# Routing and dispatch of the first mixture moved into the first attention, with the squared query norms as one fp32 product

## What is computed

```python
# first attention: 16 heads of 128
q = rmsnorm((layernorm(x) @ Wq).reshape(B, Sq, 16, 128), gq)
k = rmsnorm((ctx @ Wk).reshape(B, 64, 16, 128), gk)
v = (ctx @ Wv).reshape(B, 64, 16, 128)
x = x + tanh(g_xattn[0]) * softmax(q @ k.T * scale) @ v @ Wo
# first mixture: 64 experts, 8 a token, at most 128 tokens an expert (CAP)
n = layernorm(x)
scores = sigmoid(n @ router.T)
sc = scores + e_bias                      # 8 groups of 8 experts
# keep the 4 groups whose two best sc have the largest sum,
# then the 8 best experts in them; weights: scores / their sum * 2.5
pos = how many earlier (token, choice) pairs chose this expert
buf[expert, pos] += n[token]              # only where pos < CAP
y = (silu(buf @ w_gate) * (buf @ w_up)) @ w_down
x = x + tanh(g_ffn[0]) * (sum of weight * y of each token's experts + shared_mlp(n))
```

## Time and profile before

| | us |
|---|---|
| median of 3 runs | 1334.66 (1333.32 to 1339.74) |
| the profiled execution | 1336.93 |
| its span | 1335.2 |
| busy PE, DVE, ACT, POOL | 1038.4 (78%), 697.9 (52%), 431.5 (32%), 278.2 (21%) |
| DMA packets, moved | 58967, 66.36 MB |

### The profile page before, as it was taken

The page is one execution under the profiler, slowest core; times in us unless marked ns, Lnnn a source line. Parts: engine busy times, 40 slices in busy tenths (PEclk is TensorE's granted clock), DMA queues, the critical chain, the costliest instruction groups (busy, mean ns, idle before and its releaser), DMA issues.

```text
span 1335.2 us, 16322 instructions
## 1 busy us (share of the span) xinstructions
PE 1038.4 (78%) x5301; PEld 855.8 (64%) x5301; DVE 697.9 (52%) x1659; ACT 431.5 (32%) x793; POOL 278.2 (21%) x223
## 2 busy tenths in 40 slices
PE   5989979989766400776667368887989999999997
PEld 3867858778545300665556226564657989898996
DVE  6277586675758897222223477575675324232221
ACT  4565465554623100111111032324252232322221
POOL 0414214133000001788787110010100000000000
PEclk8999999999887655888787566757666999899899
DMA  7004000000001040788786540000000000000001
GB/s 266 3 0 137 1 1 1 0 1 1 1 0 40 24 126 11 170 173 180 166 186 120 144 164 1 2 0 0 0 0 0 1 1 0 0 0 0 0 0 64
DMA packets 58967, 66.36 MB, mean 50 GB/s; under 512 B 5037, under 2 KB 55719, under 8 KB 58151
## 3 DMA queue, kind: packets, MB, share of 16 engines
q1 hardware_dynamic: 45268, 46.48, 11.1%
q0 software_dynamic: 12288, 18.88, 8.1%
q10 hardware_dynamic: 1363, 0.37, 0.1%
HBM read 48.13 MB, written 17.56 MB: 49 GB/s over the span
## 4 chain that ended last, share of the span: by engine, by line
PE 54%; DVE 14%; issue 12%; DMA 6%; ACT 6%; POOL 6%; ACTq 0%; DVEq 0%; POOLq 0%; SPq 0%
PE bank L1959 12%; PE bank L1978 7%; DMA acc<-y,dst_now 5%; PE bank L1619 4%; PE bank L1664 4%; PE bank L1887 3%; PE bank L1845 3%; PE bank L1649 3%; POOL acc L489 2%; PE bank L1970 2%; POOL xg L479 2%; PE bank L1904 2%; POOL q_lo L468 2%; DVE cand L901 1%; PE bank L1804 1%
## 5 line engine op out<-in xcount | busy, mean ns | idle before, releaser
L1959 PE MATMUL bank<-gu_hi,xnT_split 128*128 128x352 f32 x640 | 158.7, 328 | 0.0
L468 POOL TENSOR_TENSOR q_lo<-soft,q_hi 128x512 fp32r<-128x512 f32 x64 | 93.2, 1456 | 236.8 <-ACT soft L1313 236.7
L1959 PEld LDWEIGHTS bank<-gu_hi,xnT_split 128*128 128x128 f32 x640 | 112.6, 190 | 1.0 <-issue 0.7
L479 POOL DMA_INDIRECT xg<-table,src_now x64 | 63.9, 999 | 216.5 <-DVE src_now L927 197.4
L489 POOL DMA_INDIRECT acc<-y,dst_now x64 | 102.3, 1599 | 26.7 <-issue 20.3
L1959 PE MATMUL bank<-gu_lo,xnT_split 128*128 128x352 f32 x320 | 103.8, 324 | 0.0
L1183 DVE SCALAR_TENSOR_TENSOR soft<-sg,combine_w,bank 128x176 f32<-128x176 f32 x160 | 56.4, 395 | 87.4 <-PE bank L1959 81.3
L1978 PE MATMUL bank<-dn,attnT 128*128 128x256 f32 x448 | 101.2, 384 | 0.0
L1978 PEld LDWEIGHTS bank<-dn,attnT 128*128 128x128 f32 x448 | 85.6, 194 | 11.2
L707 DVE COPY qT<-bank 128x512 f32<-128x512 f32 x64 | 44.2, 691 | 87.7 <-PE bank L1664 86.6
L1517 ACT ACTIVATE sg<-bank 128x352 f32<-128x352 f32 x80 | 37.1, 464 | 152.0 <-PE bank L1959 151.9
(11 more groups left out here) (256 smaller groups left out, 2140.1 us busy)
## 6 DMA issues: line engine op xcount, KB each, us to landing
w_gu<-in_L_ffn_w_gu SPq DMA_DIRECT2D x32, 352.0 KB
w_dn<-in_L_ffn_w_down SPq DMA_DIRECT2D x32, 176.0 KB
acc<-zeros SPq DMA_DIRECT2D x2, 2176.0 KB, 11.4
acc_rows<-acc SPq DMA_DIRECT2D x8, 512.0 KB, 4.9
gu<-in_L_gu SPq DMA_DIRECT2D x1, 3520.0 KB, 13.7
table<-xw SPq DMA_DIRECT2D x4, 640.0 KB
wo<-in_L_xattn_Wo SPq DMA_DIRECT2D x2, 1024.0 KB, 16.2
wq<-in_L_xattn_Wq SPq DMA_DIRECT2D x1, 2048.0 KB, 18.5
```

The source lines that it names most:

```text
L468: pool.tensor_tensor(q2_lo[:, h % 3, :], q2[h % 2], q2_hi[:, h % 3, :], ALU.subtract).then_inc(q2_split, 1)
L479: pool.indirect_dma_start(xg[:, q, e, :], None, table, bass.IndirectOffsetOnAxis(ap=src_now[:, q, e:e + 1], axis=0)).then_inc(xg_loaded[q] ...
L1959: mm = pe.matmul(b[:, 0:2 * F1], v[:, c, j * P:(j + 1) * P], w[:, c, p, o, :], start=(n == 0), stop=(n == len(terms) - 1))
```

## The change

In the first attention:

- the squares are made once, in fp32, and the squared norm is one fp32 product a half (two of 256 columns a head). `band_r`, `q2_hi`, `q2_lo` and POOL's subtraction are gone;
- the keys are copied by ACT, which also squares them in PSUM with a running sum (16 squares of 128 columns), in place of DVE's copy, product and sum;
- the values of group i-1, and the transposes of the keys of group i, stand inside step i;
- the 16 tiles are routed in nine batches (tile 0; 1 and 2; ... ; 15), each with a layer norm (`ln_stats`, `ln_roots`, `ln_apply`), a choice (`choose1` to `choose3`) and a place (`place`). In step i a batch `early(i)` is normed and chosen, a batch `late(i)` is normed at the step's end, chosen in step i+1, and both are placed in step i+1. Five batches (4 to 8) are placed after the last step;
- a chosen row's slot is found by a product with a triangle of ones (`earlier`) and the counts so far (`taken`), so that the search by `largest` is gone. POOL then writes each row to its slot in `table` by indirect DMAs without accumulation: eight a tile, 128 in all (`send_rows`), with a number column that names the token;
- the sigmoid is made of an exponential on ACT and a reciprocal on DVE;
- the table has 8192 slots and is filled with blank rows first (10.5 MB by SP's queue in step 0, beside the zeroed accumulators);
- normed tokens also go to DRAM (`normed_T`) and return for the shared expert, which is computed after the last place.

In the expert stage SP loads the rows of a pair with one direct DMA in place of POOL's two gathers, weights come in longer pieces (2816 bytes and 2048 bytes a partition, by a new layout made on the host, in place of 704 and 1024), and the next loads of a slot wait for `y_ready` in place of `y_full`.

The diff, cut to its core:

```diff
-                    act.activation(q2_hi[:, h % 3, :], qT[:, h % 3, :], ACT.Square)
...
-                for half in range(2):
...
-                        for n, v in enumerate((q2_hi, q2_lo)):
-                            mm = pe.matmul(n_bank[0:H0, at], band_r[:, H0 - 1 - row:2 * H0 - 1 - row],
-                                           v[:, h % 3, at], start=(h == half == n == 0),
+                        mm = pe.matmul(n_bank[0:H0, at], band[:, H0 - 1 - row:2 * H0 - 1 - row], q2[h % 2][:, at],
+                                       start=(h == half == 0), stop=(h == H0 - 1 and half == 1))
...
+BATCHES = [[0]] + [[2 * n - 1, 2 * n] for n in range(1, NT // 2)] + [[NT - 1]]
+def early(i):
+    return 2 * (i - 1)
+def late(i):
+    return 2 * i - 1
...
+            ROUTE_LATE = {1: (place, -1), 3: (choose1, 0), 4: (choose2, 0), 5: (choose3, 0), 9: (place, 0)}
+            ROUTE_EARLY = {8: ln_stats, 9: ln_roots, 10: ln_apply, 13: choose1, 14: choose2, 15: choose3}
...
+                    if i and h == 0:
+                        key_norm(i)
...
+                        if h == 12:
+                            row_stats(i + 1)
+                        elif h == 15:
+                            row_roots(EPS0)
+                            tokens_apply(i + 1)
+                if i:
+                    ln_stats(late(i))
+                    ln_roots(late(i))
+                    ln_apply(late(i))
...
+            def send_rows(b, lo, n):
+                for at in range(lo, min(lo + n, K0 * len(BATCHES[b]))):
+                    j, k = at // K0, at % K0
+                    t = BATCHES[b][j]
+                    pool.sem_inc(pool_wait_done, 1)
+                    pool.indirect_dma_start(table, bass.IndirectOffsetOnAxis(ap=slots[:, b % 2, j, k:k + 1], axis=0),
+                                            rows(t), None, bounds_check=E0 * CAP - 1,
+                                            oob_is_err=False).then_inc(row_stored[t % 8], 16)
...
+                    b = q_turn.read(act, ("keys", g, n))
+                    act.activation(ksb[:, 4 * n:4 * n + 4, :], b[:].rearrange("p (h d) -> p h d", h=4),
+                                   ACT.Copy).then_inc(keys_copied, 1)
+                    act.wait_ge(keys_copied, 4 * g + n + 1)
+                    for k in range(4):
+                        v = b[:, k * D0:(k + 1) * D0]
+                        ins = act.activation(v, v, ACT.Square, accum_out=kstat[:, 0, 4 * n + k:4 * n + k + 1])
+                    ins.then_inc(q_ring.free, 1)
...
+            def load_rows(i, q):
+                sp.dma_start(xg[:, q], table_d[:, bass.ds(8 * i + 2 * q, 2)]).then_inc(xg_loaded[q], 16)
...
-                    sp.wait_ge(y_full, 4 * i + q - 3)
+                    sp.wait_ge(y_ready, 4 * i + q - 3)
+                    load_rows(i, q)
                     load_experts(i, q)
...
-            def experts(i, last):
+            def experts(i):
                 for q in range(4):
-                    if not (last and q):
-                        pool.wait_ge(idx_now, 4 * i + q + 4)
-                        gather(i, (q + 3) % 4)
                     scatter(i, q)
```

More of the change, by code:

```diff
@@ L24 @@
 NA = 2
-ROW = DIM + E0
+TOKEN = DIM + E0
+ROW = TOKEN + 1
 H1, D1, MAIN = 16, 16, 48
@@ new lines, in _, with front, back, normed2 @@
+            for i in range(NG):
+                step(i)
+                if i == 0:
+                    ch.add(dve.memset(taken[:], 0.0))
+            m = NG - 1
+            s_turn.emptied(dve, ("scores", m, 7))
+            def front(j):
+                by_norm(m, j)
+                maximum(m, j)
+                shift(m, j)
+            def back(j):
+                sums(m, j)
+                divide(m, j)
+            def normed2(b):
+                ln_stats(b)
+                ln_roots(b)
+                ln_apply(b)
@@ L933, in experts @@
+            for j in range(G):
+                residual(2 * NG - 1, j, NG - 1, 2)
+            dve.drain().then_inc(done1["dve"], 1)
+            CH1 = ch.base + ch.k
+            for e in done1.values():
+                dve.wait_ge(e, 1)
+            sl = Chain(dve, slot_chain)
+            def experts(i):
                 qr.at(Q3, 4, i)
                 for q in range(4):
-                    if not (last and q):
-                        stage_source(i + (q + 3) // 4, (q + 3) % 4)
                     dve.wait_ge(s_ring.free, S3 + 4 * i + q + 1)
@@ new lines, in place @@
+            def place(b):
+                pe.wait_ge(sel_ready, b + 1)
+                ps = t_turn.fill(pe, ("place", b))
+                for j in range(len(BATCHES[b])):
+                    terms = [(earlier, sel[:, j * E0:(j + 1) * E0]), (ones, taken[:, b % 2, :])]
+                    if j:
+                        terms.append((ones, sel[:, 0:E0]))
+                    for k, (m, v) in enumerate(terms):
+                        mm = pe.matmul(ps[:, j * E0:(j + 1) * E0], m[:], v, start=(k == 0),
+                                       stop=(k == len(terms) - 1))
+                mm.then_inc(t_ring.full, 1)
@@ new lines, in _ @@
+            for i in range(NG):
+                step(i)
+            m = NG - 1
+            rows_across(5)
+            place(4)
+            values(m, 0, 8)
+            route(5)
+            transpose_attn1(m, 0)
+            output1(m, 0)
+            place(5)
+            transpose_attn1(m, 1)
+            output1(m, 1)
+            rows_across(6)
+            route(6)
+            transpose_attn1(m, 2)
+            output1(m, 2)
+            place(6)
+            transpose_attn1(m, 3)
+            output1(m, 3)
@@ L1587, in transpose_xn @@
+            rows_across(7)
+            route(7)
+            rows_across(8)
+            route(8)
+            place(7)
+            place(8)
+            for g in range(NG):
+                shared_in(g)
+                if g:
+                    shared_out(g - 1)
+            shared_out(NG - 1)
+            pe.drain().then_inc(done1["pe"], 1)
+            for e in done1.values():
+                pe.wait_ge(e, 1)
+            qr, sr, tr = q_ring.end(), s_ring.end(), t_ring.end()
             def transpose_xn(m):
```

1370 lines of the change are left out of this document (763 added, 607 removed).

## The result

The changed kernel took 1359.35 us in the median of 4 runs (1356.96 to 1360.77), the kernel before 1336.29 (4 runs): a ratio of 1.017, 95% interval 1.0138 to 1.0201. It is slower; the forecast of 1270 was wrong in its sign, and the time lies outside its range. The profiled execution of the changed kernel took 1358.68 us with a span of 1356.9.

What follows compares the result with a forecast made beforehand. It took PE to bound the first attention's steps, DVE the routing behind them and POOL's queue the expert stage. From a span of 1335.2 us, less 29 up to the experts and 36 in their stage, it forecast 1270, range 1230 to 1308.

Steps and rivals of the forecast that it cites:

- The price of the norm: First attention, each head on PE: fp32 norm 0.86 us in place of 0.46, plain head 3.14 in place of 2.74.
- The lockstep: Attention steps: PE and DVE both full, each head takes the longer of the two, 84.4 us for a later step's heads.
- DVE over 80% busy in steps 2 and 3: Attention steps 2 and 3: a sign named in advance that would show the forecast right.
- The joints: Between attention steps: 7.8 us for next tokens, two last heads and an output, then 6.9 for keys in step 1.
- Rival E: Attention steps: PE's clock falls, at 0.66 a step takes 143 us, 44 more in three steps, 1400 in all; chance 6%.
- Behind the last step: From the steps' end to the experts: DVE 79 us of work, 88 with waits; first expert products after 123.
- POOL's write: Rows written to the table after the steps: 1.28 us each at the gather's price, 72 writes in 92 us.
- rival B: POOL's table writes: DVE holds GpSimd up, 2.1 us a write, experts 46 us later, 1316 in all; chance 10%.
- Rival A: POOL's table writes: they cost as much as scatters, 1.87 us each, experts 29 us later, 1299 in all; chance 15%.
- Expert stage: Without gathers the accumulators' chain, landing plus 1.2 us, comes next; 174 us in place of 210, a gain of 36.
- I take 5.3: Expert stage: 5.3 us a pair, between 4.63 at the unloaded landing and 5.6 at a landing of 4.4.
- Rival C: Expert stage: pairs stay at 6.4 us since DMA engines or the wait on y_ready bind, 1305 in all; chance 9%.

Runs made afterwards that it cites:

- e2: The changed kernel with squares rounded once to fp32r and the norm made of that one half, so less exact: 1320.41 us.
- e1: The kernel before with only the fp32 norm of the change, without rounded halves and POOL's subtraction: 1371.66 us.
- e3: The changed kernel with the next tokens' norm (roots and application on DVE) at head 12 in place of head 15: 1344.5 us.
- e4: The changed kernel with ACT's copies of the transposed keys ahead of its square of head 1: 1345.69 us.
- e11: The changed kernel with the edits of e3, e4, e7 and e10 together, the norm still in fp32: 1254.04 us.
- e10: The changed kernel with batch 5's router product and its exponential ahead of the values and second exponential behind the last step: 1346.3 us.
- e6: The changed kernel with the expert weights in the old layout, pieces of 704 and 1024 bytes: 1351.92 us.
- e5: The changed kernel without the weight loads of expert pairs 4 to 31, which reuse the first four pairs' weights (timing only): 1327.49 us.
- e7: The changed kernel with four accumulators in place of two, so a scatter waits for the one of two pairs before: 1305.65 us.

## Why the prediction was wrong

**The price of the norm: too small.** "The norm of a head goes from 0.46 to 0.86 and a plain head from 2.74 to 3.14" took the fp32 price from four products of 512 columns back to back. Here there are two products of 256 columns between work of another kind. They took 0.97, and the queries before and the scores behind another 0.1 each: before, the first weight load of the norm and of the scores ran while the product before was still streaming (the scores' at 228.36 for a product at 228.47); in the kernel after the load starts with its product, behind an idle time of 0.36 to 0.42 us. In e2, with the same waits and fp32r products, the queries before the norm take 1.47 again and the scores 0.81, so the semaphores are not the reason. Nor is it a change of format as such: the scores are fp32 in every kernel, lost nothing behind the fp32r norm and lose 0.1 behind the fp32 one. Why the loads of these two do not run ahead stays open. The term is 0.71 a head and not 0.40: 45 us over 64 heads where 26 stood. e1 shows 35 net. Most of the missing 10 fits the relief from waiting for POOL's split, which the prediction costed at nothing: in the kernel before PE waited for it ten times, 7.3 us in all, and in e1 never.

**The lockstep: wrong as a mechanism, nearly right as a number.** DVE's work in step 2 was forecast as 72.5 and its busy time there is 74.8, yet it never set the pace: in heads 2 to 14 PE was busy for 66.1 of 67.5 us. The forecast for these heads, 64.5, came close because a surplus of 4 for the lockstep stood against 4 for the heads that it had too short. "DVE over 80% busy in steps 2 and 3" came out at 63 and 70%.

**The joints: the term that was left out.** The prediction gave heads 0 and 1 of step 2 13.0 us and they took 17.5; head 15 with the end of the step got 21.6 and took 33.6. With 3.0 in the middle this is all of that step's excess of 19.5. It had the keys' banks right (1.73 against 2.0 each) and counted DVE's instructions at head 15, but summed them as a maximum per head. It did not follow the chains that cross engines: choice, then roots, then tokens on DVE before PE may transpose; key roots and scaling on DVE, then the copy of head 1, then ACT's square, and only behind that ACT's copy of the keys. e3 and e4 took these chains away by order alone, 29 us as the sum of the two. With the norm's 0.31 a head too little (20 us over 64 heads) that comes to about the 48 by which the steps were too long.

**Rival E, the clock, came at a smaller size.** It was given as a fall to 0.66 over whole steps from PE's lower share. What happened is a fall behind single long waits: 0.88 over step 2. Without the waits it is 0.98 over all of the start and the steps (e11).

**Behind the last step: the waits, and the idle queue.** DVE was to reach the last place 88 after the steps' end, with 79 of work and 9 of waits; it took 102 (432.0 to its last slots at 533.87). The work was 79 as foreseen, but the waits 22.6, of which 12.5 is one that e10 removed. And "72 x 1.28 = 92" assumed that POOL, once begun, has rows most of the time: it stood idle for 21.67 us ahead of batch 5, so its last write began at 559.35, 127 after the steps' end, and not 109. The shared expert, begun at 532.4, made its last products up to 558.5, just as late, and could hide none of it.

**POOL's write: right, and rival B true in kind but small.** A write took 0.98 and 0.30 to the next, the gather's price; over all 128 the mean is 1.01 to 1.02, with DVE busy for 62% of this stretch. Rival A did not happen. Of B there is a trace: five of the 128 took 1.36 to 2.00. For instance:

```profile
361.59 1.22 DVE L836 TENSOR_TENSOR soft<-raw,small 128x1024 f32<-128x1024 f32 x1
361.65 2.00 POOL L658 DMA_INDIRECT table<-rows_b,slots  x1 [0.30 <-issue]
```

Each of the five began in the first 0.7 us of a softmax subtraction or product of 1024 columns on DVE (L822, L836), and each ended 0.84 to 0.86 us after that operation did. Writes that began beside DVE's sums and maxima of the same width (L817, L827) took 0.98. So DVE did hold POOL up, but few writes met such an operation, and all five together lost 3.9 us. The 3100 ns that the Trainium skill, "SBUF — State Buffer", section "A bandwidth-pool intuition that's wrong (but worth ruling out)", gives for such a DMA beside a DVE copy were not seen; the longest write was 2.00 us.

**Expert stage: the mechanism right, the landing mis-sized.** "The accumulators' chain is then late next: landing + 1.2" held within 0.4 (5.1 with 3.9, 6.1 with 5.1, and 4.65 with 3.8 at the unloaded end). The 3.4 that the prediction gave for an unloaded landing came from taking the 1.20 in the row for the time since the landing; it is POOL's idle time before the scatter, and the landing itself is 3.8 to 3.9 in both kernels. The step that failed is the landing of some 4.1 behind "I take 5.3", with the reason "longer pieces should lower this". The landing rose to 5.1; short pieces lowered it a little (4.8, e6), and without the weights it was 3.9 (e5). Rival C, with its 6.4 from the DMA engines, comes nearest to the time of this stage, but e7 refutes its reason: the engines carry the same pairs in 3.96 us once nothing waits for a landing.

**Sum.** The gain behind the steps is real, and in the change's own form it is used up: norm +35, the steps' other work and waits +55, routing and slots -59, expert stage -6 and the rest -3, read from the profiled executions of the kernel before, of e1 and of the kernel after. That makes +22 where the medians say +23.

## What to carry to other kernels

Price a product by the transition into and out of it, not by its back-to-back pitch; one part of a change alone, here the norm, can undo all the others. When work moves under another engine's work, sum per head only where banks give slack, and at every joint write out the chain across engines instead: moving a few lines (e3, e4, e10), with the amount of work unchanged, gave back 42 us as the sum of three runs. When the bound of a stage is removed, look for the dependent round trip behind it: doubling the accumulators was worth more than everything that the change did to that stage.

## What the runs showed of the hardware

Two fp32 products of 256 columns with a 16-column stationary operand took 0.97 us in the heads of the first attention, and the fp32r queries before and the fp32 scores behind them each 0.1 more than around fp32r norms, as the weight loads of norm and scores did not run ahead. A write by POOL that began in the first 0.7 us of a DVE product or subtraction over 1024 columns (1.22 us) ended 0.84 to 0.86 us after that; beside a reduction it was not held up (0.98). A square with a running sum of 128 columns on ACT is 0.26 us followed by a 0.19 us read of the accumulator, 0.28 from one to the next. A DMA share of 1.00 to 1.02 was reached with 251 to 261 GB/s in the expert stage (0.72 and 170 GB/s before e7's edit), with the scatters' landing at 7.0 us instead of 5.1. At a share of 0.72 the landing was already 1.3 above the 3.8 of the unloaded end, and that cost time only where a chain of waits hung on it.
